# One more pair of tiles by seven products, and sums of B formed by adding transfers

## The reference

```
h = conv1d(x, weight, groups=4, pad=4) + (cond @ c_weight.T)[:, :, None] + bias
q = h @ Wq.T                      # 16 numbers per row
scores = q @ keys.T               # 64 experts
gate = softmax over the 16 largest scores, zero elsewhere
z = (h @ A.T) * gate              # 512 numbers per row: 64 experts of rank 8
out = x + 2 * (z @ B.T)           # 1024 numbers per row
```

## Time and profile before

| | |
|---|---|
| median of 3 runs | 233.98 us (233.93 to 234.01) |
| profiled execution, its own time | 234.5 us |
| its span | 232.7 us |
| busy: PE, DVE, ACT, POOL | 224.6, 194.7, 126.3, 7.6 us |
| data moved | 40.89 MB, mean 176 GB/s |

### The profile page before, as it was taken

The page is one execution under the profiler, slowest core; times in us unless marked ns, Lnnn a source line. Parts: engine busy times, 40 slices in busy tenths (PEclk is TensorE's granted clock), DMA queues, the critical chain, the costliest instruction groups (busy, mean ns, idle before and its releaser), DMA issues.

```text
span 232.7 us, 4036 instructions
## 1 busy us (share of the span) xinstructions
PE 224.6 (97%) x1351; PEld 198.4 (85%) x1351; DVE 194.7 (84%) x443; ACT 126.3 (54%) x317; POOL 7.6 (3%) x16
## 2 busy tenths in 40 slices
PE   8999999999999999799989899999999999999995
PEld 6789998898988889688878889898898889898884
DVE  1799889999799797998999899989999896877442
ACT  4897758266491653727645584927484655252100
POOL 2010062000000000000000000000000000000000
PEclk9999999999999999999999999999999999999999
DMA  6997047749855425637360425854374156347552
GB/s 195 360 394 306 1 142 266 263 137 317 262 200 142 149 99 158 205 114 220 119 207 13 129 86 143 265 136 139 97 234 150 34 176 198 111 143 267 159 201 93
DMA packets 24869, 40.89 MB, mean 176 GB/s; under 512 B 2832, under 2 KB 11920, under 8 KB 24848
## 3 DMA queue, kind: packets, MB, share of 16 engines
q1 hardware_dynamic: 24704, 40.55, 53.6%
q10 hardware_dynamic: 144, 0.08, 0.2%
HBM read 28.04 MB, written 12.58 MB: 175 GB/s over the span
## 4 chain that ended last, share of the span: by engine, by line
DVE 58%; PE 22%; issue 14%; ACT 4%; DVEq 0%; POOL 0%; ACTq 0%; POOLq 0%
DVE x_lo L1095 9%; DVE h_t L1137 7%; DVE h_lo L1095 7%; DVE x_blk L1119 5%; PE p_z L888 5%; DVE a_raw L1266 3%; DVE zt_lo L1095 3%; DVE x_nat L1284 2%; DVE a_raw L1198 2%; DVE a_lo L1095 2%; DVE sc_b L1249 2%; DVE x_nat L1298 2%; DVE bt_lo L1095 2%; DVE e_top L1254 1%; PE p_out L937 1%
## 5 line engine op out<-in xcount | busy, mean ns | idle before, releaser
L509 ACT ACTIVATE h_hi<-h_t 128x1024 fp32r<-128x1024 f32 x16 | 17.1, 1066 | 40.0 <-DVE h_t L1137 40.0
L888 PEld LDWEIGHTS p_z<-a_hi,h_hi 128*128 128x128 f32 x240 | 32.6, 188 | 2.5 <-issue 0.3
L888 PE MATMUL p_z<-a_hi,h_hi 128*128 128x264 f32 x240 | 34.3, 285 | 0.0
L888 PE MATMUL p_z<-a_hi,h_lo 128*128 128x264 f32 x240 | 34.1, 285 | 0.0
L888 PE MATMUL p_z<-a_lo,h_hi 128*128 128x264 f32 x240 | 34.0, 284 | 0.0
L888 PEld LDWEIGHTS p_z<-a_hi,h_lo 128*128 128x128 f32 x240 | 31.2, 188 | 0.0
L888 PEld LDWEIGHTS p_z<-a_lo,h_hi 128*128 128x128 f32 x240 | 31.1, 188 | 0.0
L1095 DVE TENSOR_TENSOR x_lo<-x_blk,x_hi 128x1536 fp32r<-128x1536 f32 (+4 forms) x18 | 25.3, 1406 | 2.3 <-ACT x_hi L509 2.3
L929 PE MATMUL p_out<-b_hi,zt_hi 128*128 128x512 f32 (+1 forms) x64 | 25.0, 393 | 0.0
L930 PE MATMUL p_out<-b_hi,zt_lo 128*128 128x512 f32 (+1 forms) x64 | 24.7, 388 | 0.0
L559 ACT ACTIVATE p_conv<-p_conv,u 128x128 f32<-128x128 f32 x88 | 23.6, 356 | 1.7 <-PE p_conv L837 1.4
(11 more groups left out here) (160 smaller groups left out, 400.6 us busy)
## 6 DMA issues: line engine op xcount, KB each, us to landing
x_nat<-in_x_rows SPq DMA_DIRECT2D x16, 512.0 KB, 4.0
out_dram<-x_nat SPq DMA_DIRECT2D x31, 256.0 KB, 3.1
x_blk<-in_x_blocks SPq DMA_DIRECT2D x14, 516.0 KB, 3.6
z_dram<-a_raw SPq DMA_DIRECT2D x64, 64.0 KB, 1.8
a_raw<-z_dram SPq DMA_DIRECT2D x16, 256.0 KB, 2.9
a_raw<-in_a_wq SPq DMA_DIRECT2D x8, 264.0 KB, 7.0
x_nat<-in_b_w SPq DMA_DIRECT2D x4, 512.0 KB, 9.6
a_raw<-in_b_w SPq DMA_DIRECT2D x3, 512.0 KB, 4.2
```

Of the source, the lines that this page charges most:

```text
L509: nc.scalar.activation(dst, src, ACT.Copy).then_inc(s, 1)
L888: mm = nc.tensor.matmul(z_bank(t, b)[:, 0:HB], h[:, t % 2, r, :], a[:, r, b * HB:(b + 1) * HB], start=k == 0 and r == 0, stop=k == 2 and r ...
```

## The change

FP falls from 6 to 4, so that the tiles 4 and 5 are made as a pair too and the pairs begin two iterations earlier (five pairs instead of four). The output of tile 2 (FP - 2) is split over the iterations 4 and 5, one half each, and that of tile 3 (FP - 1) is done whole in iteration 6; before, tile 5's two halves were spread over the iterations 7 and 8. The adds and stores of these tiles move with them, one add of tile 3 to the start of iteration 7.

The sums of B are no longer made by DVE. SP loads B11 and B12 before z_out(2); POOL issues transfers that add: four from DRAM that add another block of B to a buffer, and four that add a buffer to bt_lo. ACT rounds the sum as before (bt_hi) and writes its negative, rounded, into bt_lo; the transfer then adds the sum to it, which leaves sum minus rounded sum. Both ACT instructions stand ahead of split_h(i+2) in the iteration, where bt_hi stood behind it. h_c no longer holds a block of B.

```diff
-FP = 6
+FP = 4
@@
-        b_sums = (a_raw[:, 3:5, 0:J], a_raw[:, 5:7, 0:J], h_c[:, 0].rearrange("p (a n) k -> p a (n k)", a=2))
+        b_left, b_right = a_raw[:, 3:5, 0:J], a_raw[:, 5:7, 0:J]
+        b_sums = (b_left, b_left, b_right, b_left)
@@ sync
+            sp.wait_ge(s_alo, R)
+            load_b(0, b_left, 0)
+            load_b(1, b_right, 1)
             z_out(2)
             z_in(2)
-            sp.wait_ge(s_alo, R)
-            load_b(0, 0, 0)
-            load_b(1, 0, 1)
             sp.wait_ge(s_tr, 2 * TW)
-            load_b(2, 1, 1)
...
-                if i == TB + 3:
-                    sp.wait_ge(s_btlo, 3)
-                    load_b(3, 1, 0)
@@ gpsimd
+            def sum_b(k, rows, half):
+                pool.dma_start(b_sums[k], b_w[:, 2 * rows:2 * rows + 2, half * J:(half + 1) * J], accum_op=ALU.add).then_inc(s_btsum[k], 16)
+
+            def split_bt(k):
+                pool.wait_ge(s_btneg, k + 1)
+                pool.dma_start(bt_lo[:, k], b_sums[k], accum_op=ALU.add).then_inc(s_btlo[k], 16)
+
+            pool.wait_ge(s_bt[0], 16)
+            sum_b(0, 0, 1)
+            pool.wait_ge(s_bt[1], 16)
+            sum_b(2, 1, 1)
+            split_bt(0)
+            pool.wait_ge(s_btlo[0], 16)
+            sum_b(1, 1, 1)
+            split_bt(1)
+            pool.wait_ge(s_btlo[1], 16)
+            sum_b(3, 1, 0)
+            split_bt(2)
+            split_bt(3)
@@ scalar
             def split_bt(k):
-                act.wait_ge(s_btsum, k + 1)
-                high(bt_hi[:, k], b_sums[(0, 0, 1, 0)[k]], s_bthi)
+                act.wait_ge(s_btsum[k], 16)
+                high(bt_hi[:, k], b_sums[k], s_bthi)
+                nc.scalar.activation(bt_lo[:, k], b_sums[k], ACT.Copy, scale=-1.0).then_inc(s_btneg, 1)
@@
+                if TB <= i < TB + 4:
+                    split_bt(i - TB)
                 if i in (5, 7):
                     split_w(i // 2)
                     sum_w(i // 2)
                 if i + 2 < NT:
                     split_h(i + 2)
-                if TB <= i < TB + 4:
-                    split_bt(i - TB)
@@ tensor
-                if i <= FP:
+                if i < FP:
                     out_part(i - 2, 0)
                     conv_pair(i + 2)
                     out_part(i - 2, 1)
-                elif i <= FP + 2:
-                    out_part(FP - 1, i - FP - 1)
+                elif i < FP + 2:
+                    out_part(FP - 2, i - FP)
                     conv_pair(i + 2)
+                elif i == FP + 2:
+                    out_part(FP - 1, 0)
+                    conv_pair(i + 2)
+                    out_part(FP - 1, 1)
@@ vector
-            def sum_b(k):
-                dst, other = ((0, 1), (0, 2), (1, 2), (0, 1))[k]
-                for load in ((0, 1), (2,), (), (3,))[k]:
-                    dve.wait_ge(s_bt[load], 16)
-                nc.vector.tensor_tensor(b_sums[dst], b_sums[dst], b_sums[other], ALU.add).then_inc(s_btsum, 1)
-
-            def split_bt(k):
-                dve.wait_ge(s_bthi, k + 1)
-                low(bt_lo[:, k], b_sums[(0, 0, 1, 0)[k]], bt_hi[:, k], s_btlo)
@@
-                if i <= FP + 1:
+                if i <= FP:
                     add(i - 3, 1)
+                if i == FP + 3:
+                    add(FP - 1, 1)
@@
-                if i - TB in (1, 2, 4):
-                    split_bt(i - TB - 1)
-                if TB <= i < TB + 4:
-                    sum_b(i - TB)
@@
-                if i <= FP + 1:
+                if i <= FP:
                     add(i - 2, 0)
+                elif i == FP + 1:
+                    add(FP - 2, 1)
                 elif i == FP + 2:
-                    add(FP - 1, 1)
+                    add(FP - 1, 0)
```

More of the change, by code:

```diff
@@ L153, in adaln_ffn @@
         s_xn = [sem(f"s_xn{k}") for k in range(XN)]
-        s_bt = [sem(f"s_bt{k}") for k in range(4)]
-        s_btsum = sem("s_btsum")
+        s_bt = [sem(f"s_bt{k}") for k in range(2)]
+        s_btsum = [sem(f"s_btsum{k}") for k in range(4)]
         s_bthi = sem("s_bthi")
-        s_btlo = sem("s_btlo")
+        s_btneg = sem("s_btneg")
+        s_btlo = [sem(f"s_btlo{k}") for k in range(4)]
         s_zsum = sem("s_zsum")
@@ L374, in store_half, with load_b @@
                 sp.dma_start(out[t][:, cols], x_nat[:, t % XN, cols]).then_inc(s_st[t % XN], 16)
-            def load_b(k, rows, half):
-                sp.dma_start(b_sums[(0, 1, 2, 1)[k]], b_w[:, 2 * rows:2 * rows + 2, half * J:(half + 1) * J]).then_inc(s_bt[k], 16)
+            def load_b(k, dst, half):
+                sp.dma_start(dst, b_w[:, 0:2, half * J:(half + 1) * J]).then_inc(s_bt[k], 16)
             sp.dma_start(w_raw[:, 0], conv_w[:, 0]).then_inc(s_w[0], 16)
@@ L434, in _ @@
                 m = (i - FP - 3) // 2
-                if i == TB + 3:
-                    sp.wait_ge(s_btlo, 3)
-                    load_b(3, 1, 0)
-                if i <= FP + 1:
+                if i <= FP:
                     store(i - 3, 1)
+                elif i == FP + 3:
+                    store(FP - 1, 1)
                 elif i >= FP + 4 and i % 2 == 0:
@@ L450, in _ @@
                 z_in(i)
-                if i <= FP + 1:
+                if i <= FP:
                     store(i - 2, 0)
+                elif i == FP + 1:
+                    store(FP - 2, 1)
                 elif i == FP + 2:
-                    store(FP - 1, 1)
+                    store(FP - 1, 0)
                 elif i % 2 == 0:
@@ L950, in b_sum @@
                     pe.wait_ge(s_bthi, k + 1)
-                    pe.wait_ge(s_btlo, k + 1)
+                    pe.wait_ge(s_btlo[k], 16)
                 return bt_hi[:, k], bt_lo[:, k]
@@ L1465, in _ @@
                     split_z12((i - FP - 2) // 2)
-                if i == TB + 2:
-                    split_bt(2)
                 if FP + 3 <= i < NT - 1 and i % 2:
```

## The result

The changed kernel takes 241.02 us (median of four executions, 239.47 to 241.67) against 234.0 us before: ratio 1.0285, 95% interval 1.0234 to 1.0337. It is slower, and outside my range of 229.2 to 233.3. In one experiment (order with room for two) two of ten executions took over 1.5% longer than its fastest; they are left out of its figures, and all other figures count every execution.

What follows compares the result with a forecast made beforehand. TensorE, busy 97% of the span, was taken as the bound. From the 233.98 us median, a 4.4 us gain in rounds 3 to 10 less 0.8 us of charges gave 230.4 us; 8-in-10 range 229.2 to 233.3.

Steps and rivals of the forecast that it cites:

- the term a: Time from issue to landing of one 512 KB adding transfer from POOL, taken as 5.6 us between 3.6 and 9.6.
- a up to 6.6 costs nothing: At ACT's bt_hi in round 4: ACT loses nothing if sum 1 lands before 71.6; 69.6 was expected.
- My upper row of 9.6 us: Upper bound for an adding transfer's landing, from the row of B's loads behind others at the start.
- the eight waits on POOL hold only other such transfers: On POOL: its eight waits were taken to hold back only other adding transfers; no charge.
- 2a − 13.2: ACT's stall in round 4, with h_hi and q_s behind it: up to 4 us for a from 6.6 to 8.6.
- B: Rival: slower than before, decided at ACT's bt_hi in round 4, a above 8.8; 237.2 us at a = 10; chance 0.13.
- the charge of 0.8: Transfers disturbing rounds 4 and 5: 0.4 us for DVE's subtractions, 0.4 for late x_blk; bounds 0 and 3.1.
- The table of rounds: Rounds 3 to 10, each from one scores matmul to the next, priced by old rounds: 103.48 us for 107.88.
- 1.40 from matmuls, 3.0 from gaps: Split of the 4.40 us gain in rounds 3 to 10: six fewer output matmuls, and smaller TensorE gaps.
- rival C: All transfers slow DVE's subtractions by 0.47 us and x_blk is late twice: charges 3.1, 232.7 us; chance 0.08.
- D: Rival: each POOL transfer starts only when DVE's running instruction ends; round 4 loses 1.4 us, 231.8 us; chance 0.03.
- F: Rival: pairs bind DVE in rounds 7 to 10, 231.5 us; chance counted within the forecast's 0.64.

Runs made afterwards that it cites:

- order with room for two: The changed kernel with sums taken in the order 0, 2, 1, 3 and POOL's descriptor memory doubled (2048 for 1024): 233.6 us, ratio 0.996.
- room for two: The changed kernel with the memory for POOL's transfer descriptors doubled (2048 for 1024), q_f lying in w_raw: 235.33 us, ratio 1.003.
- 7: The changed kernel with FP = 6 and outputs as before the change, adding transfers in the order 0, 2, 1, 3: 230.94 us, ratio 0.989.
- 8: The kernel of experiment 2 with only the sums as adding transfers, bt_lo subtracted by DVE: 232.44 us with FP = 4, 230.29 us with FP = 6.
- experiment 2: The changed kernel with ACT taking the sums in the order 0, 2, 1, 3 in iterations 3, 4, 5 and 7: 231.88 us, ratio 0.9932.
- experiment 4: The changed kernel with all eight POOL transfers as plain copies (accum_op left out, sums not formed): 230.01 us, ratio 0.984.
- 5: The changed kernel with each adding transfer cut to one of its two blocks (256 KB), half left without its addition: 229.63 us, ratio 0.981.
- experiment 1: The changed kernel with B's sums loaded by SP and added and split by DVE as before the change: 237.5 us, ratio 1.015.

## Why the prediction was wrong

**The step that failed is the term a**, the adding transfer, and with it "a up to 6.6 costs nothing". I took 5.6; the two that count took 7.9 and 9.4. Doubling the moving share of a plain landing was about right for the engines' time (3.15 us against 1.74) and for the shortest landing, 5.2 us, of a transfer sent at 83.52 when the DMA engines had stood still since 81 (the view of the clock has a DMA share of 0.00 from 81 to 85). But I called the queue half empty: x_blk, z and the stores run in the same rounds. I also started too low. The kernel before loads the same blocks of B into the same buffers, and its page has a row for it that I did not use:

```profile
a_raw<-in_b_w SPq DMA_DIRECT2D x3, 512.0 KB, 4.2
```

With 4.2 for 3.6 the same rule gives 6.2, already near the 6.6 up to which nothing is lost. My upper row of 9.6 us was the nearer one. By the two landings alone the stall is 17.2 − 13.2 = 4.0 us and my sum 234.4, already outside my range.

**A term was missing.** With this kernel's 1024, POOL did not send the next adding transfer before the last had landed. I wrote that "the eight waits on POOL hold only other such transfers", and looked at waits written in the code only. It cost 4.2 us here; with room for two the wait of 11.66 fell to 3.81.

**The stall's place and rule were right.** 2a − 13.2 with the measured landings is 17.2 − 13.2 = 4.0, plus 4.2 for the hold and 1.3 of delays, 9.5; round 4 was 9.3 over. B was put at a above 8.8 and given 0.13. Its own sum, with the charge of 0.8, already decides at 8.4 (2a − 13.2 = 3.6), and with the hold and the delays of 5.5 us it decides at an estimated 5.7, right beside the 5.6 that I took. So the 0.13 rested on the missing term as much as on a.

**The table of rounds was right in sum, wrong in its credit.** Without the wait 103.6 us were measured for 103.48. But "1.40 from matmuls, 3.0 from gaps" does not hold: in the kernels that form all sums and have no wait, the pair brings nothing (experiments 7 and 8), so the gain comes from DVE's relief. My own table would have said most of it: with FP = 6 and DVE relieved it gives 4 × 13.65 + 12.26 + 11.76 + 13.65 + 12.23 = 104.5, only 1.0 more. A reason, argued and not tested: the matmuls that go leave rounds that DVE's way from scores to h_t then fills. One reading in the table was off: w_lo and ws_lo of round 5, which I had put "where DVE had time", end TensorE's gap there (0.83 us in experiment 2, 0.95 and 0.96 in 4 and 5, 1.37 in 8), and the round takes 11.92 to 12.79 us for 11.76.

**The other charges.** x_blk comes late, 2.3 us of DVE's waiting where I allowed up to 1.2. What that costs shows where sum 1 holds up nothing: round 4 is 12.96 us with full adding transfers (experiment 2) and 12.12 with plain copies (experiment 4), where DVE waited 0.2 for x_blk. DVE's subtractions beside the transfers kept their length (x_lo 1.72, h_lo 1.22): rival C's first half did not occur. Nor did D: with room for two, POOL sent bt_lo 0 within 0.3 us of its copy beside a busy DVE. Nor did F: rounds 7 to 10 of the changed kernel take 51.8 us, where F had 53.3. The clock was not in my sum at all; in the profiled execution it cost at most some 0.5 us of round 5, and only because of the wait.

**What stays open.** The executions of kernels with eight full adding transfers lie 2.0 to 3.1 us apart (239.5 to 241.7 for the changed one, 230.6 to 233.1 in experiment 2), those with half the bytes added 0.5 to 1.3 (experiments 5 and 8), but those with plain copies 2.0 too, so the additions alone are not the reason. Most profiled ones are at the lower end, and no trace shows the other 1 to 2 us. A part is on record for the two kernels with the long wait: their mean granted clock over the span was 0.986 in the profiled execution and 0.978 to 0.979 in the three others, by an estimate some 3.5 us more at the lower level. In experiment 2 the clock was 1.00 in all five, so there it is something else. Whether the number of descriptors explains the hold, or another limit that the same setting moves, was not tried, nor was bt_hi behind h_hi again, with the sums in their first order.

## What to carry to other kernels

Work moved from a busy engine to transfers is free only if the first one who waits for them is off the path: write down the whole chain, with each transfer at the landing that it has beside the others, and let an engine that works in order use it an iteration later (tried here), or behind anything urgent (not tried). The same kernel was 7 us slower than before or 2 us faster by the order of four sums. And when an engine sends transfers for the first time in a kernel, ask how many it can have under way.

## What the runs showed of the hardware

An adding transfer of 512 KB from POOL held the sixteen DMA engines for 3.15 us, a copy from POOL 1.74; its issue took POOL 1.22 us against 0.72. With dynamic_dma_scratch_size at 1024 POOL never had more than one of them under way, with 2048 at least two (whether more was not seen); of plain ones and half ones the first two went out 0.4 us apart even with 1024. TensorE's clock fell to its lower level during an idle stretch of 8.65 us in the changed kernel and right after one of 2.05 us in experiment 1 (its mean over the span 0.993). It stayed at the full level after one of 2.04 us in the same execution, after one of 2.36 us with room for two, and through those of up to 1.23 us of the kernel before.
